# Moving units of a hand-ordered attention and feed-forward kernel: query units apart, token loads ahead, the first gate products into the last attention step, query weight loads issued by ScalarE

## The reference

```python
x = x + xattn(layernorm(x), ctx)       # keys and values over [ctx; tokens], 16 heads in 4 groups, head size 96
#   q = x Wq', k, v = [ctx; x] Wk', Wv'   scores = q k' / sqrt(96), softmax over 576, out = attn v, out @ Wo'
x = x + ffn(layernorm(x))
#   gate = fq(x) fq(w_gate)', up = fq(x) fq(w_up)'      h = silu(gate) * up      fq(h) fq(w_down)'
#   fq(t) = clip(round(t / s), -128, 127) * s,  s = max|t| / 127 along a row      inner width 2752
```

## Time and profile before

| what | value |
|---|---|
| median of 3 runs | 1624.09 us (1622.85 to 1625.81) |
| the profiled execution's own time | 1628.67 us |
| its span, first to last instruction | 1627.0 us |
| TensorE busy | 1528.4 us, 94% of the span |
| VectorE, ScalarE, GpSimd busy | 68%, 39%, 40% |
| mean granted TensorE clock | 0.971 of full speed |
| DMA packets' time | 73.6% of 16 engines' span |

### The profile page before, as it was taken

One profiled execution on the slowest core, in us unless ns is written; L12 is line 12 of the kernel. 1 busy time (PEld: TensorE's weight loads), 2 busy tenths in 40 slices (PEclk: granted clock), 3 DMA queues, 4 the chain that ended last, 5 costly groups with the idle time before them and its releaser, 6 DMA issues.

```text
span 1627.0 us, 23828 instructions
## 1 busy us (share of the span) xinstructions
PE 1528.4 (94%) x8033; PEld 760.8 (47%) x8033; DVE 1108.9 (68%) x2012; ACT 637.2 (39%) x1162; POOL 644.3 (40%) x843
## 2 busy tenths in 40 slices
PE   6989899999998999999999899987999999999997
PEld 3534345654444555444455444443444444444443
DVE  5254574556487565766657585775599999999984
ACT  3355455545364545545545454553111111111110
POOL 3266577545567545546845455664000000000000
PEclk9999899999999999999999999998999999999998
DMA  7298999749999965999988799989963424233331
GB/s 239 77 242 191 223 233 197 186 93 250 325 220 233 228 145 133 248 280 246 210 182 210 180 259 265 241 213 221 325 152 82 106 73 103 76 86 103 82 93 57
DMA packets 482525, 297.32 MB, mean 183 GB/s; under 512 B 405709, under 2 KB 438273, under 8 KB 481281
## 3 DMA queue, kind: packets, MB, share of 16 engines
q1 hardware_dynamic: 482433, 296.15, 73.6%
HBM read 142.61 MB, written 46.69 MB: 116 GB/s over the span
## 4 chain that ended last, share of the span: by engine, by line
PE 67%; DMA 10%; SPq 9%; DVE 5%; POOL 4%; issue 2%; ACT 1%; DVEq 0%; ACTq 0%
PE ps_s L1494 17%; PE ps_g L1507 10%; PE ps_g L871 9%; PE ps_g L872 9%; PE ps_g L873 9%; SPq L746 6%; PE ps_s L966 6%; PE ps_o L981 3%; PE ps_o L982 3%; DMA pT<-p_nat 3%; DMA xc<-x 2%; PE ps_o L984 2%; POOL p_nat L848 2%; DMA wq<-wq_c 2%; DMA dn_q<-w_t 1%
## 5 line engine op out<-in xcount | busy, mean ns | idle before, releaser
L848 POOL TENSOR_TENSOR p_nat<-p_f,p_nat 128x512 f16<-128x512 f32 x256 | 308.2, 1204 | 133.1 <-ACT p_nat L1074 133.1
L843 POOL TENSOR_SCALAR p_f<-p_f,small 128x576 f32<-128x576 f32 x256 | 201.8, 788 | 338.3 <-DVE small L1179 338.0
L1063 ACT ACTIVATE p_f<-ps_s,small 128x576 f32<-128x576 f32 x256 | 189.0, 738 | 332.8 <-DVE small L1174 329.1
L1174 DVE TENSOR_REDUCE small<-ps_s 128x1 f32<-128x576 f32 x256 | 191.5, 749 | 151.5 <-PE ps_s L967 150.2
L966 PE MATMUL ps_s<-k,q 96*128 96x512 f16 x768 | 226.1, 385 | 12.8 <-ACT p_f L1063 12.6
L1494 PE MATMUL ps_s<-w_gu_sb,xT 128*128 128x512 bf16 (+1 forms) x1152 | 226.2, 357 | 2.7 <-DVE g_sb L1593 2.7
L1526 ACT ACTIVATE g_sb<-g_sb,sx 128x512 f32<-128x512 f32 (+1 forms) x128 | 74.5, 582 | 385.5 <-DVE g_sb L1593 333.2
L1074 ACT ACTIVATE p_nat<-p_f 128x576 f16<-128x576 f32 x256 | 172.7, 675 | 76.9 <-POOL p_f L843 62.5
L1472 POOL TENSOR_TENSOR rstd<-var_eps,minus_half 128x1 f32<-128x1 f32 x16 | 8.8, 548 | 423.5 <-DVE var_eps L1548 423.5
L871 PE MATMUL ps_g<-xnT,wq 128*128 128x512 f16 x384 | 149.7, 390 | 26.7 <-DMA wq<-wq_c 17.8
L1507 PE MATMUL ps_g<-w_dn_sb,hT 128*128 128x512 bf16 x704 | 161.8, 383 | 5.3 <-DMA hT<-h_int 5.3
(11 more groups left out here) (113 smaller groups left out, 2494.4 us busy)
## 6 DMA issues: line engine op xcount, KB each, us to landing
w_in<-w_gu SPq DMA_DIRECT2D x40, 512.0 KB, 5.2
wq<-wq_c SPq DMA_DIRECT2D x36, 512.0 KB, 4.9
wo<-wo_c SPq DMA_DIRECT2D x24, 768.0 KB, 5.5
gu_q<-w_t SPq DMA_DIRECT2D x44, 256.0 KB, 4.5
w_in<-w_dn SPq DMA_DIRECT2D x8, 1376.0 KB, 7.2
x_acc<-x SPq DMA_DIRECT2D x4, 2048.0 KB, 10.6
x<-x_acc SPq DMA_DIRECT2D x8, 1024.0 KB, 6.2
x_ln<-x SPq DMA_DIRECT2D x16, 512.0 KB, 3.6
```

Of the source, the lines that this page charges most:

```text
L843: nc.gpsimd.tensor_scalar(f, f, inv_sum[:, j % 2, t:t + 1], P_UP, ALU.mult, ALU.mult).then_inc(p_scaled, 1)
L848: nc.gpsimd.tensor_tensor(h[:, S + C:2 * S], f[:, 0:T], h[:, 0:T], ALU.subtract)
L1063: nc.scalar.activation(p_f[:, tile(b, j, t) % NF, :], scores(t), ACT.Exp, bias=neg_max[:, j % 2, t:t + 1], accum_out=sums[:, j % 2, t:t + ...
L1174: nc.vector.tensor_reduce(neg_max[:, j % 2, t:t + 1], scores(t), AX.X, ALU.max, negate=True).then_inc(mx_done, 1)
```

## The change: what it does

- **Unit order** (`side_work`): the Q units of a head group no longer follow each other directly. In batches 1 to 3 the group 1 has its first unit in step 0 and the others in step 3; group 2 has them in steps 4, 6 and 6; group 3 in steps 8, 8 and 9 with output units between (batch 3: 8, 9, 10); group 0 of the next batch in steps 12, 13 and 14. Value units are in steps 1 and 2 without a Q unit, and keys begin in step 13. In batch 0, steps 0 to 6, and in batch 3 from step 10 on, and in each step 2, all side units come ahead of the value products; in the other steps after step 11, two thirds do.
- **Weight units** (`UNITS`, `WEIGHTS_IN`): 5, 17, 17, 13 units in the four batches, in batch 0 in the last 55% of it only; before 4, 16, 16, 16.
- **Splits and loads in batch 0**: split of query weights planned 14 us ahead of its use (before 8), of output weights 12 (10); every staged load up to 30 us ahead of its work (24), and 5 us of reserve behind a weight's load (1).
- **Tokens**: planned 16 us earlier for the first two tiles, 11 and 12 us for the others; the first transposes come behind the last Q unit in the plan, and the third tile's load is planned after POOL's last piece of the first.
- **Turns**: `turn_p` is planned no earlier than the value product that frees its buffer; `turn` and `keep` 1.5 us later.
- **Query weight loads**: `query_w` moves from SP to ACT, right behind the first evacuation of the Q unit that frees the half, and so goes on ACT's own DMA queue.
- **Gates**: `first_gates` becomes 4 DMAs, 6 us apart in the plan, and four of the 12 gate groups of the first token tile are multiplied in the last step of attention: three ahead of the last head's value products, one behind.

```diff
-UNITS = (4, 16, 16, 16)
-WEIGHTS_FOR = (1.0, 1.0, 1.0, 0.75)
+UNITS = (5, 17, 17, 13)
+WEIGHTS_IN = ((0.45, 1.0), (0.0, 1.0), (0.0, 1.0), (0.0, 0.75))
+FIRST_GATES = 4
...
     if b == B:
-        ahead, mine, before = (([], [], SCALES + o[2][1:5]), ([], [], o[2][5:] + o[3]))[j]
-        return [], values, labelled(b - 1, before)
+        side = labelled(b - 1, (SCALES + o[2][2:6], o[2][6:] + o[3])[j])
+        if j == 0:
+            return [], values, side
+        gates = [("G", n) for n in range(FIRST_GATES)]
+        return side[:1] + gates[:-1], values, side[1:2] + gates[-1:] + side[2:]
     if b == 0:
-        mine = {0: LATE_KEYS, 1: q[1][:1], 2: q[1][1:2], 3: q[1][2:], 4: q[2][:1], 5: q[2][1:2], 6: q[2][2:]}.get(j, [])
+        before, first = {}, {0: LATE_KEYS, 1: q[1][:1], 2: q[1][1:2], 3: q[1][2:], 4: q[2][:1], 5: q[2][1:2],
+                             6: q[2][2:] + o[0][:1]}
     else:
-        before = {0: o[2][3:], 4: o[3][:5], 5: o[3][5:]}.get(j, [])
-        mine = {1: VALUES[:3], 2: VALUES[3:] + q[1][:1], 3: q[1][1:], 5: q[2][:1], 6: q[2][1:]}.get(j, [])
+        before = {0: o[2][3:6], 1: o[2][6:], 3: o[3][:1], 4: o[3][1:4], 5: o[3][4:]}
+        first = {0: q[1][:1], 1: v[:2], 2: v[2:], 3: q[1][1:], 4: q[2][:1], 6: q[2][1:]}
...
-    n = len(side) // 3
+    n = len(side) * (2 if j > 11 else 1) // 3
     if b and j == 1:
-        n = 0
-    elif b and j == 2:
-        n = len(side) - 1
+        side, n = side[2:] + side[:2], 0
+    elif (b and j == 2) or (b == 0 and j < 7) or (b == B - 1 and j > 9):
+        n = len(side)
...
-    items = [(used(0, u) - 8, ("q", u[1], u[2])) for b, u in QUERY_USES if b == 0 and u[1]]
-    items += [(used(0, ("WO", kv, 0, h)) - 10, ("o", kv, h)) for kv in range(KV) for h in range(2)]
+            items.append((max(used(0, u) - 14.0, free + 0.5), ("q", u[1], u[2])))
+    items += [(used(0, ("WO", kv, 0, h)) - 12, ("o", kv, h)) for kv in range(KV) for h in range(2)]
...
-TOKEN_LEAD, TOKEN_STEP = 20.0, 10.0
+TOKEN_AT = (-36.0, -26.0, -11.0, -2.0)
+TOKEN_HI = (-26.5, -16.5, 9.0, 11.5)
+TOKEN_TURN = (0.3, 4.5, 16.0, 20.0)
...
-            sp.append((t + TURN, "turn_p", b, j, k))
+            free = END["PV", *divmod(b * H + j - 2, H), TT] + 0.3 if b * H + j >= 2 else 0.0
+            sp.append((max(t + TURN, free), "turn_p", b, j, k))
...
-            sp.append((filled_at(*QUERY_USES[n - 2]) + 0.3, "query_w", n))
+            act.append((filled_at(*QUERY_USES[n - 2]) + 0.2, "query_w", n))
...
+        def query_w(n):
+            (_, (_, kv, c)), slot = QUERY_USES[n], n % 2
+            filled(act, QUERY_USES[n - 2])
+            act.wait_ge(wq_kept[slot], splits_before(n, slot) * EV)
+            act.dma_start(wq2[:, slot, :, :], wq_c[kv, c]).then_inc(wq_in[slot], EV)
...
+    def gate_group(pe, t, n, x):
+        q, i = divmod(n, QU)
+        w, n0 = (w_gu0, 16 * i) if q == 0 else (w_gu, (q - 1) * GU * 4 + 16 * i)
+        nb = 16 if i < 2 else 2 * TAIL // 32
+        pe.wait_ge(gu_read, t * NUSE + (n + 1))
+        for k in range(KD):
+            mm = nc.tensor.matmul(ps_gu[n % NR][:, 0:nb * 32], x[:, k, :], w[:, n0:n0 + nb, k * 32:(k + 1) * 32],
+                                  start=(k == 0), stop=(k == KD - 1))
+        mm.then_inc(gu_done, 1)
```

More of the change, by code:

```diff
@@ L104, in side_work @@
+    side = labelled(b - 1, before.get(j, [])) + labelled(b, first.get(j, []) + then.get(j, []))
+    n = len(side) * (2 if j > 11 else 1) // 3
     if b and j == 1:
-        n = 0
-    elif b and j == 2:
-        n = len(side) - 1
+        side, n = side[2:] + side[:2], 0
+    elif (b and j == 2) or (b == 0 and j < 7) or (b == B - 1 and j > 9):
+        n = len(side)
     return side[:n], values, side[n:]
@@ L200, in weight_units @@
     for b in range(B):
+        first, last = WEIGHTS_IN[b]
         for i in range(UNITS[b]):
-            units.append((START[b] + (i + 0.4) * WEIGHTS_FOR[b] * (START[b + 1] - START[b]) / UNITS[b], ("w", g)))
+            part = first + (last - first) * (i + 0.4) / UNITS[b]
+            units.append((START[b] + part * (START[b + 1] - START[b]), ("w", g)))
             g += 1
@@ L207, in split_items @@
 def split_items():
[L209 to L210 removed]
+    items = []
+    for n, (b, u) in enumerate(QUERY_USES):
+        if b == 0 and u[1]:
+            free = filled_at(*QUERY_USES[n - 2]) if QUERY_USES[n - 2][0] is not None else 0.0
+            items.append((max(used(0, u) - 14.0, free + 0.5), ("q", u[1], u[2])))
+    items += [(used(0, ("WO", kv, 0, h)) - 12, ("o", kv, h)) for kv in range(KV) for h in range(2)]
     return items
@@ L773, in store_x, with first_gates @@
                 x2_out, EV)
-        def first_gates():
+        def first_gates(i):
             filled(sp, values_use(B - 1))
-            k = sum(1 for n, (_, what, *a) in enumerate(SP_ORDER) if what == "keep" and n < SP_ORDER.index(
-                next(e for e in SP_ORDER if e[1] == "first_gates")))
-            for i in range(2):
-                sp.wait_ge(w_stored[i], stores_before(k, i) * EV)
-            sp.dma_start(w_first[:, 0:GU * D].rearrange("p (n e) -> p n e", n=4 * GU),
-                         gu_q[0:GU].rearrange("u (i p) e -> p (u i) e", p=P)).then_inc(w_first_in, EV)
-        run = {"stage": stage, "cache": cache, "query_w": query_w, "out_w": out_w, "keep": keep,
+            turned = TURNS.index((GU - 1, 0)) + 1
+            for parity in range(2):
+                sp.wait_ge(w_stored[parity], stores_before(turned, parity) * EV)
+            first, end = i * GU // PIECES, (i + 1) * GU // PIECES
+            sp.dma_start(w_first[:, first * D:end * D].rearrange("p (n e) -> p n e", e=D // 4),
+                         gu_q[first:end].rearrange("u (i p) e -> p (u i) e", p=P)).then_inc(w_first_in, EV)
+        run = {"stage": stage, "cache": cache, "out_w": out_w, "keep": keep,
                "tokens": tokens, "turn_tokens": turn_tokens, "context": context, "residual": residual,
@@ L1095, in context_hi @@
             nc.scalar.activation(xnT_hi[:, :, T:S], ctx_in, ACT.Copy).then_inc(ctx_hi, 1)
-        run = {"split": w_split, "lift": lift, "evac": evac, "exp": chances, "high": chances_hi, "out_hi": out_hi,
+        run = {"split": w_split, "lift": lift, "evac": evac, "query_w": query_w, "exp": chances, "high": chances_hi, "out_hi": out_hi,
                "tokens_hi": tokens_hi, "context_hi": context_hi}
@@ L1510, in down @@
                 mm.then_inc(d_done, 1)
-        gates(0, True)
+        for n in range(FIRST_GATES, NUSE):
+            first_gate(n)
         gates(1)
```

86 lines of the change are left out of this document (42 added, 44 removed).

## The result

1603.4 us (median of 4 runs, 1602.1 to 1607.0) against 1623.5 us of the kernel before in the same rounds: ratio 0.9881, 95% interval [0.9858, 0.9904]. It is 1.2% faster, clear of the noise and in the direction forecast, but by 20 us where I had forecast 59; the time lies 1.4 us above the range. The profiled execution took 1603.9 us (span 1602.2, granted clock 0.989).

The account below looks back on a forecast made before the run. TensorE's work was taken to bound attention, with 104 us of idle and slow time winnable. Terms summed to 73.8 us won less 14.4 lost, net 59.4, taking the median from 1624.1 to 1565 us; range 1540 to 1602.

Parts of the forecast that it names:

- Query units apart: Seven TensorE waits for cached query weight halves, 17.8 us, go by spacing Q units and loading on ScalarE: 24 us won.
- rival 3: Queues share packet by packet: weight loads land sooner, transposes later; uncovered, half of 24 us lost, 1577; inside forecast's 0.66.
- Rival 2: ScalarE is held up by its 36 new load issues, delaying exps: 79 us lost against 59 won, 1644 us; chance 0.09.
- Weight units moved: Fewer weight units in batch 3 and early batch 0, one more in batches 1 and 2: no size of its own.
- Turns after their buffer is free: SP's 35.7 us of waits for value products are not on TensorE's path by themselves: nothing counted.
- Tokens: Earlier token loads cut score tile and output unit waits, 20.3 us with the clock: 12 us won.
- Splits in batch 0: The longer wait for DVE's query weight split, 6.7 us, goes; the first, 2.1 us, stays: 9.8 us won.
- Value products in batch 0: Value products behind side units remove most of 10.3 us of waits, 15.1 with the clock: 12 us won.
- Batch 3, 5 and 11: Wait behind batch 3's short step 6 goes, 5 us; tail waits of 21.6 us with clock shrink, 11 us won.
- DMA denser: Attention's shorter time raises DMA share to 0.95, slowing transfers; a sixth of the gain, 12.3 us, lost.
- Rival 1: The DMA engines are the bound, so waits return under other names: gain 5 to 35 us, 1604 with 20; chance 0.20.
- The price of 1.47 us for each us of waiting: In attention, 70.6 us idle plus slow clock behind stalls make 104 us, so each us of TensorE waiting costs 1.47.

Follow-up runs that it names:

- act_probe: q_on_sp plus all of ScalarE's waits and issues for the query loads, each loading only 16 bytes to a spare place: 1592.7 us, ratio 0.9808.
- weights_old: The changed kernel with the old weight unit counts (4, 16, 16, 16) and places: 1599.9 us, ratio 0.9860.
- sp_weights_old: The changed kernel with query weight loads on SP and the old weight units (4, 16, 16, 16): 1591.4 us, ratio 0.9803.
- sp_mix: The changed kernel with query weight loads on SP and weight units 5, 16, 16, 15: 1585.3 us, ratio 0.9760.
- q_on_sp: The changed kernel with the 36 query weight loads back on SP's queue, all else as changed: 1594.6 us, ratio 0.9817.
- sp_mix_tail_old: sp_mix with the old placement of value products in steps 12 to 15 of each batch (batch 3 from 10): 1597.9 us, ratio 0.9841.
- light kernels: Changed kernel and kernel before, each loading a quarter of each w_gu tile's columns and only high halves of cached query weights: 1585.2 and 1604.9 us.
- sp_mix_no_gates: sp_mix without gate groups ahead of the last output units (FIRST_GATES = 0): 1583.7 us, ratio 0.9761.

## Why the prediction was off, point by point

The direction was right, and most of the single waits did what was forecast. What failed is three steps: the second queue priced at nothing, the moved weight units without a term, and above all the sum, which added the prices as if the parts did not depend on each other.

- **Query units apart, 24 us.** The waits went to nothing, as forecast. The step that failed is beside it: I priced the second queue at nothing, with "the value products now stand later in many steps, which covers it". It is not covered: the queue costs 9 to 10 us in the old order and in the new one, near the 12 of rival 3. Rival 2 (ScalarE held) is excluded by act_probe. Of rival 3's mechanism one half is shown, transposes 1.5 us slower beside a load; the other half is wrong, since the loads land later too and not sooner. What the rival left out is that in the new order the residual's loads slow down as well (8.6 to 11.7 us).
- **Weight units moved, "counted under the last item".** A term of its own. The whole item costs some 3 us, not certain (weights_old, sp_weights_old); in it the one unit more in batches 1 and 2 loses some 9 us (sp_mix against q_on_sp) and batch 0's part wins some 6. I looked at the crowded stages it relieved and not at those it filled, where DVE is busy 64% and rows of exp waits stood already.
- **Turns after their buffer is free, 0.** Worth 12 us together with the later turns and stores of weight tiles. So the term put at nothing with "It is not on TensorE's path by itself" was mis-sized. Which of the two parts wins, and by which wait, stays open: the time that SP stands in all is the same.
- **Tokens, 12.** Worth 25 in this order. Mis-sized, since I priced only the waits of before; in the new order the old times make new ones.
- **Splits in batch 0, 9.8.** The wait went as forecast (8.8 to 2.1), by the weight units' new place; where it is back, the time is 6 us more.
- **Value products in batch 0, 12.** The waits of 10.3 us fell to 5.2 over batch 0 (and to none before 150 us), but undoing the move for the first seven steps costs 1.6 us, less than the runs can tell: right wait, wrong worth.
- **Batch 3, 5 and 11.** Batch 3 up to its tail has 2.0 us without a matmul instead of 10.7, better than forecast. In the tail the waits for chances went, even head 14's, of which I forecast that it stays; 8.3 us for exp and 4.6 for o took their place:

```profile
PE ps_s L973 <- ACT p_f L1082: 8.3, 8, 2.3
PE ps_g L878 <- DVE o L1203: 2.4, 1, 2.4
PE ps_o L988 <- DVE o L1203: 2.2, 1, 2.2
```

  (after, 1038 to 1132.6 us). 14.7 us of idle time became 13.1. Over their planned work the last six steps cost 22.0 us before and 18.9 after, so of 11 forecast 3 came. The new placement by itself won about 6 there (sp_mix_tail_old), so the idea was right and its price too high. Placed behind more work, the chances' transposes are covered, and the next step of the softmax is late.
- **New waits, 1.5.** Three waits for v_lo of 1.3 us, 3.9 in all, where I had 0.35 each; at 1.47 they are 5.7 us, just over the upper bound of 5. **Gates, 0.6 lost.** Within what the runs can tell.
- **DMA denser, 12.3 lost.** The share over the phase went from 0.90 to 0.92 and not to 0.95, and the load taken away in the light kernels is worth the same 18 us in both. So no loss of the change itself by a denser DMA is seen, beside that of the second queue. Rival 1 (engines as bound) gave the right time, 1604, by luck: by its expectation the two light kernels would have stood 40 us or more apart, and they stand 20.
- **The sum.** Adding prices item by item was itself the largest error: in us won, the order is worth -9, the times +9 and both 25. By the waits of the phase, 43.8 us left (`wq` 17.8, chances 17.7, split 6.7, q 1.6) and 29.9 came (exp 12.9, o 4.9, xnT 4.6, v_lo 3.9, x_acc 3.6): 13.9 us net where I had some 35. So a wait removed here was worth its length only where the engine that is late next had room.

Of the 39 us missing, 9 are the second queue and 9 the weight units of the middle batches: without them sp_mix wins 38 (1585.3, ratio 0.976) and is the best version with sp_mix_no_gates. The other 21 I can place only as waits: exp's row grew from 12.6 to 14.7 us there where I had halved it, and the tail, at 16 us over plan against 22.0 before, kept 5 us more than forecast. Why exp comes late in batch 1 of after is shown in part: where DVE's wait for the store behind the residual's load is gone, most of those waits are gone too (10.2 to 1.8 us). These runs move other weight units as well, and in time the difference is 3.5 us and not certain.

## What to carry to other kernels

When an order is rebuilt, test it in a two-by-two with the due times that feed it: here the order alone lost 9 us, the times alone won 9, and both won 25. Before loads go to a second queue, name the transfers that are on the path and share the time with them; here some 75 transposes took 1.5 us longer each, in the new order the residual's loads 3 us, and leaving all on one queue won 9 us. Work that is moved out of a crowded stage is priced where it arrives, too. A store that frees a buffer is better not planned right behind a large load: it took 11 us here instead of 3.7.

## What was not expected of the hardware

- 18.9 MB on a second queue, 4.1% of the engines' time, slowed some 75 transposes of the first queue from 5.3 to 6.8 us and the loads themselves from 4.8 or 4.9 to 5.5 or 6.6 us. The Trainium skill (DMA: Bandwidth & Descriptors, Queues, rings and completion order) says that each DMA engine takes turns between queues by packets. The slower transposes fit that; the single turns are not seen in these traces, and that the loads get slower too is not explained by it.
- A transpose's issue can hold SP about as long as a large transfer ahead of it runs: 10.47 us for two of them at 421.98 us, which end at 432.45, 1 us after the 2 MB load ahead has landed, and 10.05 us for one behind the gates' load, where the median of one is 1.4 us. The Trainium skill (DMA: Bandwidth & Descriptors, Queues, rings and completion order) also says that a transfer's completion is reported only after every earlier write of the same DMA engine; the store of 421.40, of 352 KB, which stood 11 us behind that load where its kind takes 3.7 us by the median, agrees with it. In before the same pair stands at 698.4 and 698.9 us, and the store took 10.2 us. No run separates the rule from plain queueing.
- The price of 1.47 us for each us of waiting was too low for this change. The phase got 23.2 us shorter (it ended at 1155.6 and 1132.4 us) with 6.4 us of gates added to it, so 29.6 us for 13.9 us of waiting less. The granted clock of its five stages went from 0.94, 0.98, 0.99, 0.97 and 0.91 to 0.97, 0.99, 1.00, 1.00 and 0.96; length by shortfall is 37.7 us before and about 14 after. I read this as the waits of 5.4 to 6.7 us that left having cost more clock than the new ones, most of them of 1 to 3 us, do; no run varies the length of a wait alone.
